# Tokens routed beside attention, a tile in each slot, and part 0 scattered during the last tiles

## What is computed

```
h = tok_ref(x)                      # five shifted patchings, x W^T + b, layernorm: 32 images x 36 patches x 192
h = concat(h, weight[x_txt])        # 32 text tokens each: 68 tokens per image, 2176 in all
h = h + attn_ref(layernorm(h))      # 12 heads of 16; scores of quantised q, k choose 32 keys, softmax of the true scores
h = h + ffn_ref(layernorm(h))
def ffn_ref(x):
    logits_fk, logits_rk = (x @ W + b) @ normalised(emb).T      # 128 experts each
    w_fk, w_rk = the 4 largest of softmax(logits), divided by their sum
    h = sum_n w_fk[n] * (x @ f_know[n])        # 192 -> 128, 4 of 128 matrices for each token
    out = sum_n w_rk[n] * (h @ r_know[n])      # 128 -> 192
```

## Time and profile before

| | |
|---|---|
| three runs | 987.56 us median (987.29 to 990.06) |
| the profiled execution | 984.25 us, span 982.4 us |
| TensorE busy | 794.3 us (81%) |
| VectorE busy | 677.0 us (69%) |
| GpSimd busy | 553.8 us (56%) |
| ScalarE busy | 324.5 us (33%) |
| chain that ended last | DVE 34%, PE 28%, POOL 17%, issue 13%, DMA 5% |

### The profile page before, as it was taken

One profiled execution on the slowest core, in us unless ns is written; L12 is line 12 of the kernel. 1 busy time (PEld: TensorE's weight loads), 2 busy tenths in 40 slices (PEclk: granted clock), 3 DMA queues, 4 the chain that ended last, 5 costly groups with the idle time before them and its releaser, 6 DMA issues.

```text
span 982.4 us, 21622 instructions
## 1 busy us (share of the span) xinstructions
PE 794.3 (81%) x6343; PEld 643.7 (66%) x6343; DVE 677.0 (69%) x4161; ACT 324.5 (33%) x887; POOL 553.8 (56%) x764
## 2 busy tenths in 40 slices
PE   5789999999999999988662288899998699589800
PEld 3778888888888777755441266799976458455800
DVE  2199999999999999984788179885453254255423
ACT  0134334444444344434631011233321146434700
POOL 5256566665666565643547475004775777775075
PEclk9789889998999789975755579999997799889955
DMA  9233453534343346301372496456799798489533
GB/s 331 93 135 129 161 184 112 180 127 163 129 168 114 112 136 219 122 23 34 93 183 71 143 289 226 154 141 176 208 393 409 266 317 297 142 293 367 180 100 92
DMA packets 81578, 177.19 MB, mean 180 GB/s; under 512 B 12952, under 2 KB 38232, under 8 KB 78648
## 3 DMA queue, kind: packets, MB, share of 16 engines
q1 hardware_dynamic: 56088, 120.62, 37.1%
q10 hardware_dynamic: 14112, 32.12, 8.8%
q0 software_dynamic: 11264, 23.09, 7.6%
HBM read 94.25 MB, written 81.53 MB: 179 GB/s over the span
## 4 chain that ended last, share of the span: by engine, by line
DVE 34%; PE 28%; POOL 17%; issue 13%; DMA 5%; ACT 1%; SPq 1%; POOLq 0%; DVEq 0%; ACTq 0%
DVE work L1356 12%; DVE top L1350 9%; PE bank L1216 6%; POOL early L742 5%; PE bank L1199 4%; PE bank L1214 4%; POOL slots_g L749 3%; POOL slots_x L720 3%; PE bank L1264 3%; PE bank L1266 2%; DMA early<-slots_x 2%; DVE s_hit L1520 2%; PE bank L1250 2%; PE bank L965 1%; DVE place L1626 1%
## 5 line engine op out<-in xcount | busy, mean ns | idle before, releaser
L1356 DVE MATCH_REPLACE8 work<-top,work 128x68 f32<-128x68 f32 x896 | 179.3, 211 | 0.0
L1350 DVE MAX8 top<-work 128x8 f32<-128x68 f32 x896 | 128.9, 213 | 6.6 <-ACT tru L792 6.2
L1626 DVE COPY place<-bank 96x512 f32<-96x512 f32 x98 | 66.0, 685 | 82.3 <-PE bank L1199 81.6
L742 POOL DMA_INDIRECT early<-slots_h,s_all x68 | 65.6, 964 | 87.4 <-DMA slots_h<-m_y 67.0
L1635 DVE COPY place<-bank 128x256 f32<-128x256 f32 x98 | 40.9, 423 | 92.8 <-PE bank L1250 91.5
L965 PE MATMUL bank<-early,xp 128*128 128x192 f32 x432 | 94.0, 381 | 6.5 <-DMA xp<-in_a_x 5.0
L965 PEld LDWEIGHTS bank<-early,xp 128*128 128x128 f32 x432 | 90.5, 233 | 8.6 <-DMA xp<-in_a_x 5.3
L742 POOL DMA_INDIRECT early<-slots_y,s_all x68 | 66.3, 975 | 52.7 <-DMA slots_y<-m_y 30.5
L1199 PE MATMUL bank<-ident,early 128*96 128x128 f32 x392 | 68.2, 301 | 25.4 <-DMA early<-slots_x 25.4
L672 POOL TENSOR_TENSOR sc<-work,tru 128x476 f32<-128x476 f32 x32 | 38.0, 1189 | 87.5 <-ACT work L827 87.5
L720 POOL DMA_INDIRECT slots_x<-early,s_all x68 | 67.7, 996 | 31.6 <-issue 18.4
(11 more groups left out here) (187 smaller groups left out, 1729.5 us busy)
## 6 DMA issues: line engine op xcount, KB each, us to landing
early<-slots_x SPq DMA_DIRECT2D x49, 384.0 KB
slots_y<-m_y ACTq DMA_DIRECT2D x49, 384.0 KB
slots_h<-m_y ACTq DMA_DIRECT2D x49, 256.0 KB
early<-slots_g SPq DMA_DIRECT2D x49, 256.0 KB, 4.8
f_all<-in_f_know SPq DMA_DIRECT2D x16, 768.0 KB, 9.8
r_all<-in_r_know SPq DMA_DIRECT2D x16, 768.0 KB, 15.3
slots_x<-zero SPq DMA_DIRECT2D x28, 360.0 KB, 3.0
slots_x<-zero SPq DMA_DIRECT2D x28, 336.0 KB, 3.3
```

The lines of the kernel that those rows point to most:

```text
L742: nc.gpsimd.indirect_dma_start(g_in[:, i % DEPTH, k, 0:width], None, src, bass.IndirectOffsetOnAxis(s_all[:, r - 1, i, k:k + 1], 0)).then_ ...
L1350: last = nc.vector.max(top8[:, c, :], work[:, par, c, :])
L1356: last = nc.vector.match_replace(work[:, par, c, :], top8[:, c, :], work[:, par, c, :], TAKEN)
L1626: nc.vector.tensor_copy(m_flat[u][0:HALF, :], turn_bank[u][0:HALF, :]).then_inc(sem["m_xt0"], 1)
```

## The change

Routing is moved into attention's slots. `LOAD_AT` says in which slot a tile is loaded: tile 0 in slot 18, tile 1 in slot 20, then one in each slot from 21 to 35. A tile's stages follow over four slots: statistics on VectorE (b), norm, transpose and query (b+1), logits, choice and one-hot (b+2), position (b+3). The patch products are eight a slot and end with slot 20; `keep_busy` has five products instead of ten in slots 22 to 31. Part 0's counts are formed in slot 31, its searches run in slots 32 and 33 (`FIND_AT`), its sends in the steps from slot 32 on (`SEND_AT`). `find_slots` takes two tiles at a time. The counts move through a carried row (`first_row` times `place`) instead of an accumulation kept in PSUM. Eight chunks of `f_all` (7 to 14) are loaded in slots 22 to 29, and the first products start with them; chunks 0 and 1 come after the last tile's load, chunks 2 to 6 beside the first groups. In the diff, after the tables, come SyncE, GpSimd (`route` closes each slot), TensorE and VectorE.

```diff
-FIRST, LAST = 4, 24
+FIRST, LAST = 4, 22
-SEARCH = 11
-LATE = 13
+LATE = 15
-    EMBED_AT.setdefault(_n // 8 if _n < 48 else 6 + (_n - 48) // 7, []).append((2 + _n // CHUNKS_K, _n % CHUNKS_K))
+    EMBED_AT.setdefault(_n // 8, []).append((2 + _n // CHUNKS_K, _n % CHUNKS_K))
+TAIL = 14
+NEEDS = tuple(((i + 1) * P - 1) // S for i in range(NT))
+LOAD_AT = {18: 0, 20: 1, **{19 + _i: _i for _i in range(2, NT)}}
+ROUTED = max(LOAD_AT) + 4
+BASE_AT = 31
+FIND_AT = {BASE_AT + 1: ((0, 1), (1, 2), (3, 2)), BASE_AT + 2: ((5, 2), (7, 2))}
+SEND_AT = {BASE_AT + 1: (0, 1, 2), BASE_AT + 2: (3, 4), BASE_AT + 3: (5,), BASE_AT + 4: (6,), BASE_AT + 5: (7,), BASE_AT + 6: (8,)}
...
-            return main + spill if g == 0 else spill + main
+            return main[EARLY:LATE] + main[:EARLY] + main[LATE:] + spill if g == 0 else spill + main
...
+                if b in LOAD_AT:
+                    load_h1(LOAD_AT[b])
...
-            for c in range(EARLY):
+            for c in range(2):
                 load_f(c)
...
-                    if g == 0 and LATE + n < CHUNKS:
-                        load_f(LATE + n)
+                    if g == 0 and 2 + n < EARLY:
+                        load_f(2 + n)
+                    if g == 0 and n == EARLY:
+                        sp.wait_ge(sem["t_pos"], NT)
+                        sp.wait_ge(sem["tiles_known"], 2)
+                        load_f(LATE)
...
+            def route(b):
+
+                if b - 2 in LOAD_AT:
+                    t_one_hot(LOAD_AT[b - 2])
+                if b in LOAD_AT:
+                    t_rstd(LOAD_AT[b])
+                for i in SEND_AT.get(b, ()):
+                    send(i)
...
+            def keep_busy(i):
+
+                bank_free(i)
+                for n in range(5):
+                    nc.tensor.matmul(routed_in(i)[:], lower_b[:], zero[:, 0:256].bitcast(BF16), start=True, stop=True)
...
+                if b - 2 in LOAD_AT:
+                    t_logits(LOAD_AT[b - 2])
+                if b - 3 in LOAD_AT:
+                    t_position(LOAD_AT[b - 3])
...
+                if LAST_EMBED + 1 < b < BATCH:
+                    keep_busy(LOAD_AT[b - 1])
+                if b - 1 in LOAD_AT:
+                    t_turn(LOAD_AT[b - 1])
...
+                if b - 1 in LOAD_AT:
+                    t_query(LOAD_AT[b - 1])
...
                 if take:
                     take8(b, par, 1)
+                if b - 2 in LOAD_AT:
+                    t_choose(LOAD_AT[b - 2])
...
                 if take:
                     take8(b, par, 2)
+                if b in LOAD_AT:
+                    t_stats(LOAD_AT[b])
+                if b == BASE_AT:
+                    form_counts(0)
+                for i, n in FIND_AT.get(b, ()):
+                    find_slots(0, i, n)
...
+            for n in range(PART_GROUPS[0]):
+                turned_first(FIRST_GROUP[0] + n)
+                if n < 4:
+                    find_slots(0, PARTS[1][0] + 2 * n, 2)
+                if n == 4:
+                    form_weights()
+                if n in (6, 9, 12, 15, 18):
+                    first = (n - 6) // 3 * 2
+                    find_slots(1, first, min(2, PARTS[0][1] - first))
+
+            def sum_and_find(n):
+                first_sum(n)
+                if n % 2 == 0:
+                    find_slots(1, PARTS[1][0] + n, 2) if n < 8 else None
+
+            beside(turned_first, 1, range(*PARTS[0]), sum_and_find)
```

More of the change, by code:

```diff
@@ L893, in _ @@
[L893 removed]
+            slot(BATCH + 1, 1)
+            for b in range(BATCH + 2, ROUTED):
+                if b - 2 in LOAD_AT:
+                    t_query(LOAD_AT[b - 2])
+                if b - 3 in LOAD_AT:
+                    t_placed(LOAD_AT[b - 3])
+                if b - 1 in LOAD_AT:
+                    t_norm(LOAD_AT[b - 1])
+                    t_turned(LOAD_AT[b - 1])
+                if b - 2 in LOAD_AT:
+                    t_exped(LOAD_AT[b - 2])
             act.wait_ge(sem["t_weights"], 1)
[L895 removed]
+            nc.scalar.activation(e_all, e_all, ACT.Exp).then_inc(sem["t_weights"], 1)
@@ new lines, in t_turn, with t_query @@
+            def t_turn(i):
+                pe.wait_ge(sem["t_norm"], i + 1)
+                bank_free(i)
+                for c in range(2):
+                    last = nc.tensor.transpose(routed_in(i)[0:HALF, c * P:(c + 1) * P], xn_of(i)[:, c * HALF:(c + 1) * HALF], ident[:])
+                last.then_inc(sem["t_turn"], 1)
+            def t_query(i):
+                pe.wait_ge(sem["t_xt"], i + 1)
+                for c in range(2):
+                    last = nc.tensor.matmul(routed_in(i)[:, 0:P], w_rt[:, c, :], t_xT[0:HALF, i % 2, c, :], start=(c == 0), stop=(c == 1))
+                last.then_inc(sem["t_qmm"], 1)
@@ L1147, in count_part @@
-            def count_part(g):
-                last = PARTS[g][1] - 1
-                pe.wait_ge(sem["t_placed"], last + 1)
-                nc.tensor.matmul(bank[3 + g][:, 0:2 * NE], lower_b[:], t_hot[:, last % 3].rearrange("p r n -> p (r n)"), start=False, stop=True,
-                                 skip_group_check=True).then_inc(sem["base_products"], 1)
-            def turn_counts(g):
-                pe.wait_ge(sem[f"base_steps{g}"], 1)
-                for q in range(2):
-                    last = nc.tensor.transpose(bank[1][:, q * P:(q + 1) * P], count[:, g, q, :], ident[:])
-                last.then_inc(sem["base_products"], 1)
@@ L1182, in _ @@
-            route_in_turn(slot, t_step)
+                if b - 1 in LOAD_AT:
+                    t_query(LOAD_AT[b - 1])
+                if b == BASE_AT:
+                    sum_counts(0)
+                if b == BASE_AT + 1:
+                    name_tiles(0)
+            slots_of(pe, slot)
+            slot(BATCH + 1, 1)
+            for b in range(BATCH + 2, ROUTED):
+                if b - 2 in LOAD_AT:
+                    t_logits(LOAD_AT[b - 2])
+                if b - 3 in LOAD_AT:
+                    t_position(LOAD_AT[b - 3])
+                if b - 1 in LOAD_AT:
+                    t_turn(LOAD_AT[b - 1])
+                    t_query(LOAD_AT[b - 1])
@@ L1409, in _, with form_counts @@
             norm(1, 1)
+            part_steps = [Steps(dve, f"base_steps{g}", 8) for g in range(2)]
+            def form_counts(g):
+                st = part_steps[g]
+                st.start(0)
+                dve.wait_ge(sem["base_products"], 3 * g + 1)
+                st.done(nc.vector.tensor_scalar(ntile_i[:, 0], bank_of_base(g)[:, 0:4:2], float(HALVED), None, ALU.add))
+                st.wait()
+                st.done(nc.vector.tensor_scalar(ntile_i[:, 1], ntile_i[:, 0], 6, None, ALU.logical_shift_right))
+                st.wait()
+                st.done(nc.vector.tensor_scalar(ntile[:], ntile_i[:, 1], -1.0, 0.0, ALU.add, ALU.max))
+                st.wait()
+                st.done(nc.vector.tensor_copy(ntile_b[:], ntile[:].unsqueeze(2).to_broadcast([P, 2, NE])))
@@ new lines, in form_base @@
+            def form_base(g):
+                st = part_steps[g]
+                first, end = PARTS[g]
+                mine = base[:, 2 * g:2 * g + 2]
+                nc.vector.tensor_copy(idf[:, first:end], idx[:, first:end, :, 0:K4])
+                dve.wait_ge(sem["base_products"], 3 * g + 2)
+                st.done(nc.vector.tensor_tensor(mine, bank_of_base(g)[:, 0:2 * NE].rearrange("p (q n) -> p q n", q=2),
+                                                iota_e[:].unsqueeze(1).to_broadcast([P, 2, NE]), ALU.subtract))
+                st.done(nc.vector.tensor_copy(ends[:, 2 * g:2 * g + 2], bank_of_base(g)[:, 2 * NE:2 * NE + 2]))
+                st.wait()
+                st.done(nc.vector.tensor_scalar(mine, mine, float(HALVED), float(HALVED * (NE - 1)), ALU.mult, ALU.add))
+                st.wait()
+                for q in range(2 * g, 2 * g + 2):
+                    last = nc.vector.tensor_scalar(ended[:, SPILL_AT[q]:SPILL_AT[q] + SPILLS[q]], iota_t[:, 0:SPILLS[q]], ends[:, q:q + 1], None, ALU.is_ge)
+                st.done(last)
```

587 lines of the change are left out of this document (254 added, 333 removed).

## The result

The changed kernel took 1026.4 us (median of four runs, 1006.4 to 1046.8) against 987.7 for the kernel before. The ratio is 1.021, 95% interval 1.016 to 1.026, from the two quicker runs (some 21 us above the kernel before); the slower two, 1041.1 and 1046.8, which spent more time at a lower TensorE clock, are not in it. So it is slower, where I had predicted 971 and allowed up to 992. The profiled execution is the fastest of the four, at 1006.44 us.

A forecast was written before the change was run, and what follows sets the result against it. VectorE was taken to pace attention, a relay of short steps routing, TensorE the products. Start 23.1 us earlier, +0.5 and +6 for products: -16.6 from the profiled 984.25 gives 967.7, so 971 us as median; range 955 to 992.

The forecast's parts named there:

- my 6.5: Parts 0 and 1: growth of the products from searching two tiles at a time, +0.5 and +6 us.
- VectorE's work in the slots: Attention slots 18 to 31: statistics, choices and part 0's counts lengthen VectorE's work by 26.6 us, with nothing hiding it.
- Eight chunks: Slots 6 to 20: eight patch chunks instead of seven, mostly hidden behind VectorE, +3 us (0 to 9).
- TensorE in slots 21 to 31: Routing added, five keep-busy products dropped: some slots late, +5 us, less 4.4 us regained after patch products, net +0.6.
- The 5 us for such slots: Slots 21 to 31: total allowed for some slots where a falling granted clock makes TensorE late.
- From slot 32 to the first products: End of routing: GpSimd's queue of 36 sends decides; first products 71.0 us after slot 32 begins, where before needed 124.3.
- The port rule of the Trainium skill: Sends of slots 32 and 33 would wait up to some 20 us for VectorE; the sum assumed no wait.
- The first products: Parts 0 and 1: double searches outlast TensorE's work in hand; +0.5 us in part 0, +6 in part 1.
- The f chunks: Five instead of three chunks loaded beside the first groups: 0 us in the sum, given four groups of look-ahead.
- The clock rival: Slots 21 to 31: less filler and waits for `o` drop TensorE to 1.2 GHz, making it the bound; 1011 us, chance 0.19.

The follow-up runs named there:

- all three edits: Changed kernel with searches one tile at a time, ten keep_busy products instead of five, and a tile's choice moved behind `ek` and `o`: 966.1 us, ratio 0.977.
- the pair of experiments with and without filler: Changed kernel with choice behind `o` and ten keep_busy products, double searches kept: 995.8 us; with ten fp32 products added ahead of multiplications awaiting a double search: 975.3 us.
- single searches: Changed kernel with searches one tile at a time, one in each of part 0's groups and none beside part 1's sums: 1007.9 us.
- the one with filler from slot 21 on: Changed kernel with one-tile searches, choice behind `ek` and `o`, and ten keep_busy products starting at slot 21 instead of 22: 967.4 us, ratio 0.980.

## Why the prediction was wrong

Against the profiled time of my sum, 967.7 us, the profiled execution, 1006.4, is 38.7 us late (by chance the same figure as that of the medians). The first products start 9.1 us later than forecast (544.6 against 535.5), parts 0 and 1 take 247.6 us instead of 215.9 (209.4 and my 6.5), 31.7 more, and what follows is 1.9 shorter than before. Two steps failed, both for the same reason: TensorE's clock.

- **VectorE's work in the slots**, 26.6 us: right. At full clock a slot with a tile takes 13.8 us with all three edits (forecast 13.7).
- **Eight chunks**, +3: hidden. Slot 18 came 2 us earlier than before, slot 21 at 307.5 against the 311.6 of my sum.
- **TensorE in slots 21 to 31**, net +0.6: the first failed step. From slot 21 to 32 were 167.2 us instead of 152.9. I counted the five dropped products as 1.8 us saved; they were what brought the clock back after a fall, as the kernel before shows without any routing. The 5 us for such slots rested on slot 24's 15.43 us as a slot at half clock, but that slot had been only partly at half clock (0.75; this is its window in the kernel before):

```profile
342.20:357.60 15.40, 15.36 (x112) 11.70 (x112) 13.52 (x97) 5.15 (x15) 9.00 (x15) 0.75 0.03 8
```

  A whole one is 20.4 us with routing, against the 17.8 in the rival. I also read VectorE as busy 96 to 99% all through attention; in the 40.2 us at 0.75 it was busy 36.43, 91%, so there TensorE had set the pace. The wait for `o`, named there, was real: 11.0 us in six waits.
- **From slot 32 to the first products**, 71.0 us: right, 69.9 measured. First send after 10.9 us (forecast 10.5), 36 sends within 54.3 us (55.0), landing 2.33, load 3.20.
- **The port rule of the Trainium skill** (page "SBUF — State Buffer", section "Who interferes with whom") had no effect of that size in the trace: from 485.5 to 498.0 VectorE is busy 11.53 of 12.5 us, and the sends take 0.96 to 1.13 us, one about every 1.27 us. I had also read the rule too widely. In the Trainium skill the lock belongs to VectorE's two-port modes, which copies and `tensor_scalar` can enter, and to instructions with two SBUF inputs beside a GpSimd instruction that reads SBUF; a search is for the most part `SCALAR_TENSOR_TENSOR`. So the trace does not speak against that rule.
- **The first products**, +0.5 and +6: the step that failed most, 31.7 us. I priced the double searches as stalls, "2 us each", by VectorE's surplus over the work in hand, and the six long waits are indeed 2.4 to 4.1 us. I wrote "the clock's ramp being the same", though the kernel before had 0.93 there with waits for copies of at most 0.9 us, and loses it when its searches are merely paired (0.71). With each long wait came 7 to 24 us at 1.2 GHz; by the pair of experiments with and without filler, some 60% of the loss comes by way of the clock.
- **The f chunks**, 0: right for the most part; single searches alone brought part 0 from 128.3 to 115.6 us. The 3.7 us above the 111.9 of before, and part 1's 2.8 to 7.7 above 97.5, were not traced to a cause.
- **The rivals.** The clock rival had the right mechanism, with a chance of 0.19, but I looked for it only in the slots, not in the products, where most of the loss lies; its 1011 us lies near the profiled 1006 in part by luck, since all 45 us of it are in the slots. The clock falls after a wait of 2.46 us and stays up with filler in that wait. The Trainium skill, page "TensorE: Matmul & The Clock Gate", section "What's actually happening", has throttling as the default state, which activity releases; with that the trace agrees. That a busy engine alone is enough would not fit the rows: 100.67 of 102.60 us busy at 0.50.

In sum, the gain of the change was there, and two losses of clock, of which neither belongs to its idea, took it about twice over; with the three edits it takes 966 us, 23.3 less than before. The stages that the sum had right show there: the first transpose comes at 533.4 (forecast 535.5), and what follows the products takes 212.6 us (214.4 before). That parts 0 and 1 then take 216.2 us, against the 215.9 of my sum, is chance: my 6.5 us were for double searches, and this kernel has none.

## What to carry to other kernels

Before filler products are dropped or work is put ahead of something TensorE waits for, price the stage at both clock levels, and take the low level from a stretch that is low all through. Work on another engine beside a stream of products should be cut into pieces shorter than the products in hand; where two pieces must be joined, products without use in the wait can pay for themselves. Runs of one kernel that spread by several per cent, as here from 1006 to 1047 us, can be a sign that some stage runs now at one clock level and now at the other; compare stages, and not only totals.

## What the runs showed of the hardware

The clock stayed low under full load: 102.60 us at 1.2 GHz with TensorE busy 98% of them, where five more bf16 products a slot gave 0.91. Waits of 2.4 and 2.5 us in an otherwise full stream of fp32 products came with 23.9 and 17.1 us at 1.2 GHz. The state is not fixed by the program: the same slots ran at 0.74 in one profile (changed kernel) and at 0.58 in another (single searches), 156 against 182 us. A long wait is not the only thing that a low stretch follows: in slot 23 of the kernel before and in slot 25 of the one with filler from slot 21 on, one began with no long wait ahead of it. Why, and why a low stretch ends where it does, these runs don't show.
